# Two-layer graph kernel on one core: node-type embedding products made in the opening stage and kept as six rows, normalised tiles buffered in the place of the second count slab

## Chip, cores and metric

The kernel runs on one core of a Trainium2 chip. The metric is the device time of one execution in microseconds (us). The engines are named PE (TensorE, matmul), PEld (its weight load), ACT (ScalarE), DVE (VectorE), POOL (GpSimd) and SP (SyncE, which only starts DMA transfers). ACT and POOL can start transfers too.

## What is computed

There are 1250 nodes with 768 features, 40000 edges (src, dst, an edge type out of 3) and a node type out of 3. The first block is graph attention with 12 heads of 64, the second one three relational graph convolutions. In front of these the normalised features (768 columns) are joined with an embedding of the node's type (128 columns), so that their first weight matrices have 896 rows.

```
x = layernorm(x + gat(x, W_fc, attn_l, attn_r, W_res, src, dst))
h = concat([x, node_emb[node_type]], -1)                 # 768 + 128
for layer in (1, 2, 3):                                  # rgcn_conv
    xw  = einsum('nd,rde->rne', h, w_rel)                # 3 relations
    msg = xw[edge_type, src] * inv[dst, edge_type]       # inv: 1 / count
    h = relu(segment_sum(msg, dst) + h @ w_root + bias)
x = layernorm(x + h)
```

## The kernel before

It has three stages, and each is a block at whose end the engines meet.

**Counting** (`count_matrices`) turns the edge lists into three matrices of counts, 1250 by 1250, one for each relation, and stores them in DRAM as `ct`. DVE first prepares the edges (keys, one-hot rows `oh_rem`, a table of ranges); when the table has come back through a transfer, PE starts on its windows (L405, L421), and ACT empties them into `ct_stage` (L351). PE transposes some small weights ahead of that (L385 to L392). ACT has nothing to do until the first window is full. Between the small transposes and the first window PE has nothing to do either.

**Attention** (`attention`) runs 12 heads times 10 tiles of 125 nodes. For each of these 120 units DVE, ACT and POOL form the weights `pw` (L774, L687, L692, L647), and PE adds up `head_sums` (L849). At the end of a head ACT copies the sums to `oT`, PE turns them (`turn_sums`, L857), DVE divides (L779 to L784), and POOL adds the result to `res` (L654). `turn_sums` of a head stands behind the sixth unit of the next one. Only for head 10 it stands behind the last unit, directly ahead of that of head 11.

**Relational layers** (`rgcn_layers`) work with float32 matmuls that are split in two parts (high and low): ACT makes the high part (a cast), DVE the low part (a subtraction). So weights `w_raw` become `w_hi` (L1221) and `w_lo` (L1342), and a right-hand side `gs` or `accT` becomes `g_hi` and `g_lo` (L1233, L1364). A step multiplies one block of 128 weight rows with a group of 418 or 416 nodes (`product`, L1101, three matmuls for each 128 outputs). Steps of a relation first sum over the neighbours (`aggregate`, L1073). `STEPS` lists them; in the first group the seven root steps come first, then relation 0, 1, 2. Each engine's program goes through `STEPS` in this order, with the work for a later step written between.

What stands at the head of the layers, before:

- SP loads four blocks `emb_raw` (the last 128 rows of the root and relation weights, L993), then the `w_raw` blocks in order, with two buffers: block j waits for the low part of block j-2 (L1011).
- POOL loads the biases (L1033), then the count slab of relation 0 (`inv` and `ct_in`, L1041, L1043). The second slab's place is at first taken by `emb_raw`, so its load waits for the embedding products. Then POOL stores the ten normalised tiles (L1050).
- PE multiplies `emb_raw` with `emb_cols`, the transposed embedding repeated three times (`embed`, L1110); ACT casts these products to `emb_w` (L1212) and DVE subtracts (L1335) to give the low parts.
- DVE normalises `res` + x, two tiles at a time (`first_norm`: L1304, L1308, L1312, L1314, ACT's square root L1197, L1317, L1324). The results are `x1`, three buffers for ten tiles. A fourth tile waits until the first has been stored.
- For each tile PE transposes `x1` in two halves (`turn_x1`, L1123), ACT keeps them in `accT` (L1206), and ACT and DVE make its high and low part `h_hi` (L1201) and `h_lo` (L1329). Four tiles come before the first step, two more with each of steps 0, 2 and 4. Group 0 needs the first four tiles, and the aggregation needs all ten.

```
if t >= 3:                                   # first_norm: x1 has three places
    dve.wait_ge(x1_out[t % 3], 16 * (t // 3))
```

## Time and profile before

| | us |
| --- | --- |
| median of 3 executions | 2479.14 |
| lowest, highest | 2478.87, 2480.29 |
| the profiled execution, by the clock of the others | 2480.09 |
| its span, first to last instruction | 2478.3 |
| attention, end of the last `res` addition | 814.1 |
| first `product` of the layers | 866.4 |
| first `aggregate` of the layers | 916.3 |

The span is the sum to work with; 1.8 us lie outside it. A row of the timeline names start, length, engine, line, operation and tiles. The square bracket at its end is the idle time of this engine before it and the work that ended it. The chain of work is followed back from the last instruction.

### The profile page before, as it was taken

To read this page: it belongs to the slowest core of one execution; us is meant where nothing else is said; L and a number is where in the kernel's file an instruction comes from. 1 tells how busy PE (TensorE), PEld (TensorE's weight loads), DVE (VectorE), ACT (ScalarE), POOL (GpSimd) and SP (SyncE) were. 2 spreads that over 40 slices of the span, in tenths; PEclk is the share of its full clock that TensorE was granted. 3 is DMA by queue.
4 is the path that set the end of the run, shared out by engine and by line. 5 is a ranking of instruction groups with operands and counts; after the bars stand their busy time and mean duration, and the time that the engine had idled before them with its cause. 6 is when DMAs were issued, how large, how long until landed. Compare 5 with 4: busy or idle time off the path is not lost.

```text
span 2478.3 us, 29974 instructions
## 1 busy us (share of the span) xinstructions
PE 2173.8 (88%) x10953; PEld 1837.3 (74%) x10954; DVE 1228.3 (50%) x1882; ACT 780.9 (32%) x1062; POOL 451.2 (18%) x378
## 2 busy tenths in 40 slices
PE   3998761888888389999999999999999899999997
PEld 1555440333333179999999999999999899999997
DVE  7887656999995452233333342232333342344335
ACT  0133332888886231121221231121221231212212
POOL 0000001899999200000000000000000000000000
PEclk9999885999999589999999999999999999999999
DMA  0133332211110523333423423333323423335332
GB/s 17 42 86 88 89 91 59 89 32 32 32 32 16 159 90 88 99 90 105 121 83 114 113 71 89 97 106 110 117 77 108 123 66 103 121 102 139 100 99 78
DMA packets 138639, 215.04 MB, mean 87 GB/s; under 512 B 87580, under 2 KB 87818, under 8 KB 138513
## 3 DMA queue, kind: packets, MB, share of 16 engines
q1 hardware_dynamic: 99179, 147.28, 21.1%
q0 software_dynamic: 39344, 66.16, 9.3%
q8 instruction: 80, 1.31, 0.2%
q14 instruction: 36, 0.29, 0.0%
HBM read 182.38 MB, written 30.62 MB: 86 GB/s over the span
## 4 chain that ended last, share of the span: by engine, by line
PE 58%; DMA 5%; DVE 2%; ACT 2%; issue 0%; SPq 0%; ACTq 0%; DVEq 0%
PE banks L1101 30%; PE banks L1073 27%; DMA w_raw<-in_L_gnn_w_root_dram 3%; DVE w_lo L1342 1%; ACT w_hi L1221 1%; DMA s_x<-x_tiles 1%; PE banks L1136 1%; DMA emb_raw<-in_L_gnn_w_rel_dram 0%; PE banks L1110 0%; PE banks L1123 0%; PE banks L1154 0%; DVE h_lo L1373 0%; ACT accT L1249 0%; DVE tail_stats L1392 0%; DVE back L1390 0%
## 5 line engine op out<-in xcount | busy, mean ns | idle before, releaser
L1073 PE MATMUL banks<-ct_in,h_hi 125*128 125x416 f32 (+1 forms) x1710 | 604.5, 353 | 0.6 <-ACT accT L1206 0.6
L1073 PE MATMUL banks<-ct_in,h_lo 125*128 125x416 f32 (+1 forms) x1710 | 603.2, 353 | 0.0
L1101 PE MATMUL banks<-g_hi,w_hi 128*128 128x416 f32 (+1 forms) x1440 | 518.4, 360 | 21.6 <-DVE g_lo L1364 21.5
L1101 PE MATMUL banks<-g_lo,w_hi 128*128 128x416 f32 (+1 forms) x1440 | 513.7, 357 | 0.0
L1101 PE MATMUL banks<-g_hi,w_lo 128*128 128x416 f32 (+1 forms) x1440 | 513.4, 357 | 0.0
L1342 DVE TENSOR_TENSOR w_lo<-w_raw,w_hi 128x768 fp32r<-128x768 f32 (+1 forms) x228 | 227.9, 1000 | 468.2 <-ACT w_hi L1221 468.2
L1221 ACT CAST w_hi<-w_raw 128x768 fp32r<-128x768 f32 (+1 forms) x228 | 197.8, 868 | 449.8 <-PE banks L1101 354.6
L1073 PEld LDWEIGHTS banks<-ct_in,h_lo 125*128 125x128 f32 x1710 | 323.7, 189 | 4.4
L1073 PEld LDWEIGHTS banks<-ct_in,h_hi 125*128 125x128 f32 x1710 | 322.5, 189 | 4.1 <-ACT accT L1206 0.8
L1237 ACT CAST g_hi<-gs 128x416 fp32r<-128x416 f32 (+3 forms) x180 | 97.5, 542 | 702.7 <-DVE gs L1352 702.7
L849 PE MATMUL head_sums<-pw,x 125*65 125x512 f32 x720 | 273.0, 524 | 51.5 <-POOL pw L647 35.2
L647 POOL TENSOR_TENSOR pw<-y,csum 125x1250 f32<-125x1250 f32 x120 | 313.9, 2658 | 16.0 <-PE head_sums L849 8.1
L1352 DVE TENSOR_TENSOR gs<-banks,inv 128x416 f32<-128x416 f32 (+3 forms) x180 | 106.6, 592 | 393.4 <-PE banks L1073 393.4
L1101 PEld LDWEIGHTS banks<-g_hi,w_hi 128*128 128x128 f32 x1440 | 276.4, 192 | 29.9 <-DVE w_lo L1342 20.1
L1101 PEld LDWEIGHTS banks<-g_hi,w_lo 128*128 128x128 f32 x1440 | 276.9, 192 | 3.5
L1101 PEld LDWEIGHTS banks<-g_lo,w_hi 128*128 128x128 f32 x1440 | 275.4, 191 | 3.5
L1041 POOL DMA_DIRECT2D inv<-s_inv x27 | 15.4, 571 | 1386.6 <-DVE gs L1352 1373.8
L849 PEld LDWEIGHTS head_sums<-pw,x 125*65 125x65 f32 x720 | 93.4, 139 | 223.8 <-issue 158.9
L294 DVE TENSOR_SCALAR oh_key<-iota_key,edge_cols,minus_window 125x750 bf16<-125x750 uint16 x516 | 212.4, 477 | 79.1 <-PE win L421 55.9
L421 PE MATMUL win<-oh_key,oh_rem 125*128 125x375 bf16 x1032 | 201.9, 341 | 11.4 <-issue 7.8
L774 DVE SCALAR_TENSOR_TENSOR y<-spreads,a_high,low_spread 125x1250 f32<-125x1250 f32 x120 | 180.7, 1516 | 33.5 <-POOL pw L647 21.3
L762 DVE CUSTOM_DVE_ANT_0 junk<-spreads,nbr 125x1250 bf16<-125x1250 f32 x120 | 171.5, 1452 | 32.1 <-PE spreads L816 32.1
(189 smaller groups left out, 1538.5 us busy)
## 6 DMA issues: line engine op xcount, KB each, us to landing
w_raw<-in_L_gnn_w_rel_dram SPq DMA_DIRECT2D x117, 384.0 KB, 3.3
ct_in<-s_ct POOLq DMA_DIRECT2D x18, 2031.2 KB, 28.1
w_raw<-in_L_gnn_w_rel_dram SPq DMA_DIRECT2D x54, 448.0 KB, 3.9
ct_in<-s_ct POOLq DMA_DIRECT2D x9, 2041.0 KB, 28.4
s_ct<-ct_stage SPq DMA_DIRECT2D x30, 610.4 KB
w_raw<-in_L_gnn_w_root_dram SPq DMA_DIRECT2D x39, 384.0 KB, 3.2
w_raw<-in_L_gnn_w_root_dram SPq DMA_DIRECT2D x18, 448.0 KB, 5.8
low_spread<-s_low SPq DMA_DIRECT2D x12, 610.4 KB
```

The lines of the kernel that those rows point to most:

```text
L294: nc.vector.tensor_scalar(oh_key[:, p, b], iota_key[:].rearrange("e s r d -> e (s r d)"), edge[:, 1, bass.ds(c, 1)], minus_w[:, bass.ds(w, ...
L421: ins = nc.tensor.matmul(win[:, p, m, 0:BANK * KEY], oh_rem[:, bass.ds(q, 1), :, b].rearrange("e q s -> e (q s)"), oh_key[:, p, b, m * BAN ...
L647: nc.gpsimd.tensor_tensor(pw[:, u % 3], y[:, u % YS], csum[:, u % NT], ALU.mult).then_inc(weighed, 1)
L762: nc.vector.tensor_tensor_reduce(junk[:, u % 2], a1[:, 0:N], nbr[:, t], 1.0, -NOEDGE / 10, ALU.subtract, ALU.max, tops[:, u:u + 1]).then_i ...
L774: nc.vector.scalar_tensor_tensor(out=y[:, u % YS], in0=r1, scalar=a1_high[:, s, h:h + 1], in1=lowb[:, h % 2], op0=ALU.add, op1=ALU.max).th ...
L849: ins = nc.tensor.matmul(po[:, o:o + w], x[:, s, h], pw[:, u % 3, o:o + w], start=s == 0, stop=s == NT - 1)
L1073: ins = nc.tensor.matmul(pb[0:rows, PA, 0:s.w], a, b, start=j == 0, stop=j == len(pairs) - 1)
L1101: ins = nc.tensor.matmul(pb[:, m, 0:s.w], a, b, start=s.first and j == 0, stop=s.last and j == len(parts) - 1)
L1221: nc.scalar.copy(w_hi[:, s.wi % WS, 0:s.mt * 128], w_raw[:, s.wi % 2, 0:s.mt * 128]).then_inc(w_hi_done, 1)
L1237: nc.scalar.copy(g_hi[0:rows, s.gi % 2, 0:s.w], gs[0:rows, 0:s.w]).then_inc(g_hi_done, 1)
L1342: nc.vector.tensor_tensor(w_lo[at], w_raw[:, s.wi % 2, 0:s.mt * 128], f32(w_hi[at]), ALU.subtract).then_inc(w_lo_done, 1)
L1352: nc.vector.tensor_tensor(gs[0:rows, 0:s.w], pb[0:rows, PA, 0:s.w], inv[0:rows, s.slab % 2, 0:s.w], ALU.mult).then_inc(gs_done, 1)
```

## The change

Six parts.

1. **Embedding products in the counting stage.** ACT loads `emb_raw` (four transfers behind the edge lists). PE transposes the embedding, ACT copies it three times, and PE makes the four products, one for each root or relation matrix, into the PSUM place of the windows. The low part is made by PE and ACT: PE adds minus the high part (`minus_rows`, three rows of minus the identity) onto the product, and ACT casts what is left. Only six rows, three high and three low, are stored to DRAM (`emb`). PE goes on to the windows when the last low part is done.
2. **In the layers** POOL sets `emb_w` to zero, ahead of its first slab load, and SP brings the six rows back in three transfers. The four `emb_raw` loads, `embed` on PE, ACT and DVE, and their waits are gone.
3. **`x1` gets eight places** instead of three: five new ones (`x1_more`) lie where the second slab goes. Only tiles 8 and 9 wait for a place. The second slab's load waits until tiles 3 to 7 are stored, transposed and split. SP stores the tiles, between its weight loads.
4. **Order at the head of the layers.** DVE normalises four tiles in a row; their low parts `h_lo` come behind the first right-hand side. ACT loads the square root table first, and makes `h_hi` of the four tiles behind the first `g_hi`.
5. **The wait for the biases** stands at the first output instead of at the head.
6. **At the end of attention** `turn_sums` of head 10 moves from behind the last unit to behind the sixth unit of head 11. The embedding's load, transpose and copies there are gone.

```diff
@@ count_matrices, scalar @@
+            act.wait_ge(raw_in, 48)
+            for q in range(R + 1):
+                rows = io["L1_gnn_w_root1"][D:D1, :] if q == 0 else io["L1_gnn_w_rel1"][q - 1, D:D1, :]
+                act.dma_start(emb_raw[:, q], rows).then_inc(emb_w_in, 16)
+            act.wait_ge(emb_turned, 1)
...
+            high(0)
+            for q in range(1, R + 1):
+                high(q)
+                low(q - 1)
+            low(R)
...
+            act.wait_ge(emb_out, 32)
             act.wait_ge(consts, 10)
@@ count_matrices, tensor @@
+            products(0)
+            for q in range(1, R + 1):
+                products(q)
+                rest(q - 1)
+            rest(R)
+            pe.wait_ge(emb_low, R + 1)
             pe.wait_ge(u_ready, 4)
@@ attention, tensor @@
-                if h == H - 1 and s == 3:
-                    pe.wait_ge(small_in, 48)
-                    pe.wait_ge(shared, H - 2)
-                    nc.tensor.transpose(turned_emb, emb, ident[0:R, 0:R]).then_inc(emb_turned, 1)
-            pe.wait_ge(emb_kept, 3)
-            turn_sums(H - 2)
+                if s == 5 and h == H - 1:
+                    turn_sums(h - 1)
             turn_sums(H - 1)
@@ rgcn_layers @@
+X1_GROUP = [0] * 3 + [1] * (NT - 5) + [2] * 2
+X1_STORES = {1: (0, 1), 2: (2, 3), 4: (4, 5), 6: (6, 7), 8: (8, 9)}
...
+            nc.gpsimd.memset(emb_w[0:TY].bitcast(F32), 0.0).then_inc(emb_zero, 1)
             load(0)
+            pool.wait_ge(x1_out[1], 16 * X1_GROUP.count(1))
+            pool.wait_ge(xt_turned, 2 * (NT - 2))
+            pool.wait_ge(h_lo_done, NT - 2)
             load(1)
-            for t in range(NT):
-                pool.wait_ge(normed, t + 1)
-                pool.dma_start(dram["x1"][t * T:(t + 1) * T, :], x1[t % 3]).then_inc(x1_out[t % 3], 16)
```

What DVE does at the head of the layers, from the first normalisation on, before (`x1_tiles` and `accT` are the places of `x1`):

```order
L1324 TENSOR_SCALAR x1_tiles<-res,norm_mean_var,norm_var_eps 125x768 x2
L1335 TENSOR_TENSOR emb_w<-banks,emb_w 3x896 x4
L1342 TENSOR_TENSOR w_lo<-w_raw,w_hi 128x896 x2
L1329 TENSOR_TENSOR h_lo<-x1_tiles,h_hi 125x768 x2
L1304 SCALAR_TENSOR_TENSOR res<-res,x 125x768
```

and, further on in the same program, around the first `g_lo`:

```order
L1324 TENSOR_SCALAR x1_tiles<-res,norm_mean_var,norm_var_eps 125x768
L1329 TENSOR_TENSOR h_lo<-accT,h_hi 125x768
L1329 TENSOR_TENSOR h_lo<-x1_tiles,h_hi 125x768
L1364 TENSOR_TENSOR g_lo<-accT,g_hi 128x418
L1342 TENSOR_TENSOR w_lo<-w_raw,w_hi 128x896
```

Now, at the same second place, with the fourth tile's normalisation as the first row:

```order
L1368 TENSOR_SCALAR x1_more<-res,norm_mean_var,norm_var_eps 125x768
L1380 TENSOR_TENSOR w_lo<-w_raw,w_hi 128x896
L1402 TENSOR_TENSOR g_lo<-accT,g_hi 128x418
L1380 TENSOR_TENSOR w_lo<-w_raw,w_hi 128x896
L1373 TENSOR_TENSOR h_lo<-x1_tiles,h_hi 125x768 x2
L1373 TENSOR_TENSOR h_lo<-accT,h_hi 125x768
L1373 TENSOR_TENSOR h_lo<-x1_more,h_hi 125x768
L1380 TENSOR_TENSOR w_lo<-w_raw,w_hi 128x896
L1348 SCALAR_TENSOR_TENSOR res<-res,x 125x768
```

Four `h_lo` moved from ahead of the first `g_lo` to behind it, and stand now ahead of the third weight block's `w_lo`.

SP's transfers at the head of the layers, before:

```order
L993 DMA emb_raw<-in_L1_gnn_w_root1_dram 128x896
L993 DMA emb_raw<-in_L1_gnn_w_rel1_dram 128x896 x3
L1011 DMA w_raw<-in_L1_gnn_w_root1_dram 128x896 x6
L1011 DMA w_raw<-in_L1_gnn_w_rel1_dram 128x896 x36
```

and now:

```order
L1064 DMA w_raw<-in_L1_gnn_w_root1_dram 128x896 x2
L1046 DMA s_x1<-x1_tiles 125x768 x2
L1064 DMA w_raw<-in_L1_gnn_w_root1_dram 128x896
L1068 DMA emb_w<-s_emb 3x3584 x3
L1046 DMA s_x1<-accT 125x768
L1046 DMA s_x1<-x1_more 125x768
L1064 DMA w_raw<-in_L1_gnn_w_root1_dram 128x896 x2
L1046 DMA s_x1<-x1_more 125x768 x2
L1064 DMA w_raw<-in_L1_gnn_w_root1_dram 128x896
```

The first two weight blocks stand at the front, and the third stands behind two stores of `x1`.

## Rows read from the trace of the kernel before

**Rows 1.** Chain that ended last, head of the layers: start us, length us, what

```profile
815.74 9.54 DMA emb_raw<-in_L_gnn_w_rel_dram
825.32 7.61 PE banks L1110 x16
833.01 3.31 ACT emb_w L1212 x4
840.73 21.51 DMA s_x<-x_tiles
...
876.73 6.97 PE banks L1101 x21
896.49 5.58 PE banks L1101 x21
...
916.34 5.63 PE banks L1073 x20
```

**Rows 2.** Timeline of POOL: a memset in attention, bias loads of the layers

```profile
761.39 1.14 POOL L665 MEMSET hot_rows<- 3x1250 f32 x1
...
814.94 2.91 POOL L1033 DMA_DIRECT2D bias_cols<-in_L_gnn_b_dram  x3 [0.85 <-POOLq L508]
```

**Rows 3.** Timeline of the layers' head, DVE, ACT, PE

```profile
824.67 0.96 DVE L1304 SCALAR_TENSOR_TENSOR res<-res,x 125x768 f32<-125x768 f32 x1 [12.19 <-DMA bias_cols<-in_L_gnn_b_dram]
...
828.94 0.17 DVE L1314 TENSOR_SCALAR norm_var_eps<-norm_mean_var 125x2 f32<-125x2 f32 x1
...
838.02 1.28 ACT L1197 ACT_TABLE_LOAD   x1
...
839.75 1.27 DVE L1324 TENSOR_SCALAR x_tiles<-res,norm_mean_var,norm_var_eps 125x768 f32<-125x768 f32 x2
...
847.18 1.82 DVE L1329 TENSOR_TENSOR h_lo<-x_tiles,h_hi 125x768 fp32r<-125x768 f32 x2
...
862.27 0.68 DVE L1324 TENSOR_SCALAR x_tiles<-res,norm_mean_var,norm_var_eps 125x768 f32<-125x768 f32 x1 [7.76 <-DMA s_x<-x_tiles]
...
863.00 1.51 PE L1123 MATMUL banks<-ident,x_tiles 125*128 125x125 f32 x6 [6.92 <-DVE x_tiles L1324]
...
866.37 0.69 PE L1101 MATMUL banks<-g_hi,w_hi 128*128 128x418 f32 x1 [1.86 <-DVE g_lo L1364]
...
866.47 1.09 DVE L1342 TENSOR_TENSOR w_lo<-w_raw,w_hi 128x896 fp32r<-128x896 f32 x1 [0.24 <-ACT w_hi L1221]
```

**Rows 4.** Loads by line or tile: four of `emb_raw`; two of `w_raw`, issued 846 to 848

```profile
DMA to landing us min/median/max: 3.2/5.1/9.5
...
DMA to landing us min/median/max: 9.4/10.4/11.3
```

**Rows 5.** Timeline of the end of attention

```profile
795.95 3.00 DVE L750 TENSOR_SCALAR hot_rows<-nbr,kind_col 64x1250 fp32r<-64x1250 f32 x1
...
801.25 2.31 PE L849 MATMUL head_sums<-pw,x 125*65 125x512 f32 x6 [0.60 <-POOL pw L647]
...
803.40 2.30 PE L857 MATMUL spreads<-wfcT,res 65*125 65x65 f32 x20
...
807.16 4.00 PE L857 MATMUL spreads<-wfcT,res 65*125 65x65 f32 x20 [1.46 <-DVE x L784]
```

**Rows 6.** Loads by tile: four `w_raw` issued 961 to 984, beside a `ct_in` load

```profile
DMA to landing us min/median/max: 3.3/7.2/7.9
```

**Rows 7.** The page's part on DMA issues: tile, queue, count, size, median us to landing

```profile
ct_in<-s_ct POOLq DMA_DIRECT2D x18, 2031.2 KB, 28.1
```

**Rows 8.** Timeline of the counting stage's opening

```profile
6.01 0.94 DVE L206 CAST edges_raw<-edges_raw 80x1500 f32<-80x1500 int32 x1 [5.86 <-DMA edges_raw<-in_edge_type_dram]
...
12.83 0.17 DVE L227 COPY attnT<-scores 64x24 f32<-64x24 f32 x1 [1.36 <-PE scores L389]
...
44.12 0.19 PE L405 MATMUL win<-zero_a 125*128 125x1 bf16 x2 [30.06 <-DVE table L278]
...
66.32 1.28 ACT L351 ACT_TABLE_LOAD   x1 [66.32 <-PE win L405]
```

More of the change, by code:

```diff
@@ L53 @@
 A1_K = 2 * H
+KH = D1 // 128
+TY = 64 + R
 ROWS = [(0, 418), (418, 416), (834, 416)]
 def count_matrices(nc, io, dram, csum, nbr, a1_high, a1_low, a2_col, a_rows, under, stored, proj_out, rows_out, ident):
-    stage, csf, xs, xT, res, iota_key, row, rowp, num = under
+    stage, csf, xs, xT, res, iota_key, row, rowp, num, emb_raw, emb_w = under
     with ExitStack() as ctx:
@@ L393, in _, with products, rest @@
                              start=True, stop=True).then_inc(u_sum, 1)
+            pe.wait_ge(emb_in, 16)
+            nc.tensor.transpose(tp[:, 2, 0:R], emb[:], ident[0:R, 0:R]).then_inc(emb_turned, 1)
+            pe.wait_ge(emb_kept, 3)
+            pe.wait_ge(emb_w_in, 16 * (R + 1))
+            pe.wait_ge(minus_set, 1)
+            half = D1 // 2
+            def products(q):
+                if q >= 2:
+                    pe.wait_ge(emb_low, q - 1)
+                for c in range(2):
+                    ins = nc.tensor.matmul(win[0:TY, q % 2, c, 0:half], emb_cols[:], emb_raw[:, q, c * half:(c + 1) * half],
+                                           start=True, stop=False, skip_group_check=True)
+                ins.then_inc(emb_done, 1)
+            def rest(q):
+                pe.wait_ge(emb_high, q + 1)
+                for c in range(2):
+                    ins = nc.tensor.matmul(win[0:TY, q % 2, c, 0:half], minus[32:32 + R], emb_w[32:32 + R, q, c * half:(c + 1) * half],
+                                           start=False, stop=True, skip_group_check=True)
+                ins.then_inc(emb_rest, 1)
+            products(0)
[4 more added lines that the diff above has]
+            pe.wait_ge(emb_low, R + 1)
             pe.wait_ge(u_ready, 4)
@@ L948, in halves_of_chunk, with rgcn_layers @@
     return ((s.g - 1) * 4 + at // 5, at % 5) if 0 <= at < 20 else None
-def rgcn_layers(nc, io, dram, out, ident, accT, back, emb_w, g_hi, g_lo, gs, bias, hot, hot_rows, emb_cols, many,
-                x, res, h_hi, h_lo, ct, emb_raw, w_hi, w_lo, w_raw, inv, x1_pair):
-    x1 = [x1_pair[:, 0], x1_pair[:, 1], accT[0:T, KX, 0:D]]
+def rgcn_layers(nc, io, dram, out, ident, accT, back, emb_w, g_hi, g_lo, gs, bias, hot, hot_rows, many,
+                x, res, h_hi, h_lo, ct, w_hi, w_lo, w_raw, inv, x1_pair, x1_more):
+    x1 = [x1_pair[:, 0], x1_pair[:, 1], accT[0:T, KX, 0:D]] + [x1_more[:, i] for i in range(NT - 5)]
+    x1 += x1[0:2]
     f32 = lambda ap: ap.bitcast(F32)
@@ L990, in _, with store_x1 @@
         def _(sp):
-            for q in range(R + 1):
-                src = io["L1_gnn_w_root1"][D:D1, :] if q == 0 else io["L1_gnn_w_rel1"][q - 1, D:D1, :]
-                sp.dma_start(emb_raw[:, q], src).then_inc(emb_in, 16)
+            def store_x1(t):
+                sp.wait_ge(normed, t + 1)
+                sp.dma_start(dram["x1"][t * T:(t + 1) * T, :], x1[t]).then_inc(x1_out[X1_GROUP[t]], 16)
             def load_back(c):
@@ L1011, in _ @@
                 sp.dma_start(w_raw[:, j % 2, 0:s.mt * 128], weights_of(s)).then_inc(w_in[j % 2], 16)
+                if j == 2:
+                    sp.wait_ge(emb_zero, 1)
+                    for c in range(3):
+                        sp.dma_start(emb_w[c * 32:c * 32 + R].bitcast(F32), dram["emb"][c % 2]).then_inc(emb_in, 16)
+                if j in X1_STORES:
+                    for t in X1_STORES[j]:
+                        store_x1(t)
                 if s.i == HEADS_OF[2]:
                     for b in range(3):
-                        sp.wait_ge(x1_out[b], 16 * ((NT + 2 - b) // 3))
+                        sp.wait_ge(x1_out[b], 16 * X1_GROUP.count(b))
                     for c in range(4):
@@ L1493, in build @@
         h_lo = t("h_lo", [T, NT, D1], F32R)
-        attention(nc, io, dram, x, res, share, oT, (a1_high, a1_low, a2_col, a_rows), csum, csum16, nbr, y, stored, proj_out, rows_out, (hot, hot_rows, emb_cols, many), ident)
+        attention(nc, io, dram, x, res, share, oT, (a1_high, a1_low, a2_col, a_rows), csum, csum16, nbr, y, stored, proj_out, rows_out, (hot, hot_rows, many), ident)
         ct0 = t("ct_in0", [T, NT, WIDE], F32R)
-        with sb("emb_raw", [128, R + 1, D1], F32) as emb_raw:
+        with sb("x1_more", [T, NT - 5, D], F32) as x1_more:
             pass
```

136 lines of the change are left out of this document (64 added, 72 removed).

## Prediction, written before the changed kernel ran

> **What bounds the kernel now.** I read the chain that ended last first. From 916.34 us on it is PE almost without a break, and this change alters nothing there: the same steps, the same matmuls. Ahead of that the chain leaves PE for a long time, and there the change works. At the head of the layers it goes through the load of `emb_raw` (9.54 us), the embedding products on PE (7.61), ACT's casts of them (3.31), and a store of a normalised tile (21.51) [rows 1]. So from the end of attention at 814.1 (POOL waits 0.85 before 814.94, [rows 2]) to the first product at 866.37 [rows 3] PE has little to do but the work that the change takes out. The reader should see three different waits: DVE's first normalisation waits 12.19 us for the biases, ACT's square root stands behind the casts until 838.02, and the fourth tile waits for the store of the first (7.76 us) [rows 3]. Taking one away would uncover the next; the change takes away all three. So the question is what is late next, and I follow that chain forward.
>
> **The head of the layers, up to the second product.** The engines leave attention at about 814.4 (its own gain comes later).
>
> DVE's statistics of two tiles take from 824.67 to 829.11, 4.44 us [rows 3], so they end at 818.8. ACT splits two weight blocks before the root. These are now SP's first transfers. The four `emb_raw` loads of the same size, which stood there, landed 3.2 us after issue at best and 5.1 in the middle [rows 4], so the second block lands at 819 to 820, its cast (0.85: two of them lie between 833.01 + 3.31 = 836.32 and 838.02, [rows 1, 3]) ends near 820.2, and the root follows. The table load (1.28 us) now runs while the weights are on their way. From the end of the table load at 839.30 to the first tile at 839.75 it is 0.45: tile 0 could start at 820.6.
>
> POOL now sets `emb_w` to zero just there, from 817.85. The nearest row is a memset of 1250 elements in 1.14 us [rows 2]; 3584 elements in proportion make 3.3 us, until 821.1. Does that hurt DVE? A DVE operation of the same form as the normalisation took 3.00 us for 1250 elements beside POOL's work, 2.4 ns each [rows 5]; the normalisation alone takes 0.68 for 768, 0.9 ns each [rows 3]. So such an operation is slowed beside POOL, and I take 0.8 us for it, between 0 and 3.3. The Trainium skill (SBUF — State Buffer, the part on the engine and DMA sides) says that VectorE in a two-port mode and GpSimd hold a common port pair exclusively, the loser waiting for the whole instruction. By that rule tile 0 would start at 821.1 or later, 0.5 us more than without; the slow row agrees with its direction, but its POOL neighbour read memory and a memset doesn't.
>
> Tiles 0 and 1 take 1.27, so 822.7. Then 4.44 for the next two statistics and 0.45 for the root: tile 2 at 827.6, tile 3 at 828.2, DVE free at 828.9. Before, tile 3 started at 862.27 and the first product at 866.37, 4.10 later [rows 3]; now tile 2 is transposed directly ahead of it (1.51 us for a tile, [rows 3]), so the first product comes at 828.2 + 4.1 + 1.5 = **833.8**, 32.6 earlier.
>
> That isn't the gain. The first product was followed by a gap, and the next one came at 876.73 [rows 1], bound by DVE: from the start of the third block's `w_lo` at 866.47 [rows 3] it is 10.26 us. Now four `h_lo` (1.82 for two, 3.64 in all, [rows 3]) stand ahead of that `w_lo`: 833.8 + 1.1 (the second block's `w_lo`, 1.09) + 3.6 gives 838.5 on DVE. The other side is the third block itself. SP issues it when the first `w_lo` is done, 828.9 + 1.1 = 830.0. With a slab load in flight such loads took up to 7.9 us [rows 6], and 9.4 to 11.3 with stores too [rows 4]. Here two `x1` stores stand ahead of it in SP's own queue and the slab (issued at 821.7) is in flight, so I take 8.5: landed 838.5, cast 0.94 later, `w_lo` starts at 839.5, and the second product at **849.8**. That is 26.9 us earlier. Bounds: by DVE alone 848.8 (27.9); without the memset's effect 1 us more (28.9); with 11.3 us of loading 852.6 (24.1).
>
> From the second product to the first aggregation it was 916.34 - 876.73 = 39.6 us [rows 1], with products, transposes and norms in the same order as now. Stores of tiles 4 to 9 went by POOL and go by SP now; the fourth and fifth weight blocks stand behind stores 2 and 3 in that queue while the slab is landing. The fifth one is waited for by ACT in the chain to tiles 6 and 7. I take 0.7 us for it, from 0 to 3. The sum for the head is 26.9 - 0.7 = **26.2** (21 to 29).
>
> What is moved off the path and stays covered: the first slab's load is 3.3 us later and lands about 28 us after 821.7 [rows 7], near 851, against an aggregation at 890; the second slab waits until tile 7 is turned, about 882, lands near 911, and is needed one relation (some 50 us) after 890. The six rows of `emb_w` are needed only with the seventh step. The biases are needed only at the first output. These cost nothing.
>
> **The end of attention.** The last unit's matmuls end at 803.56, then `turn_sums` of head 10 takes 2.30, ACT copies the last head in 1.46 including hand-over, and the last `turn_sums` takes 4.00 [rows 5]. Now the first of these lies behind unit 6. PE has 0.6 us of slack for each unit there [rows 5], so of its 2.3 us some 0.5 are left at the last unit: gain 2.30 - 0.5 = 1.8. The same twenty rows took 2.30 at one place and 4.00 at the other; if the last one keeps the faster pace, 1.7 more. I take the middle, **2.6** (1.8 to 3.5).
>
> **The opening.** PE's windows start at 44.12, behind the range table, after 30.06 us of idling; ACT is idle until 66.32 [rows 8]. ACT's four loads are issued from 6.0 on (the edge lists' arrival, [rows 8]). The same loads took about 10.4 us from the first issue to the last landing (814.4 to 824.8, [rows 1, 4]): 16.5. Four products and four corrections are two matmuls each. PE did eight matmuls of this size in 7.61 [rows 1], so sixteen take 15.2; I allow 24 for a slower pace; ACT's casts are 0.83 each [rows 1], of which three stand in PE's way, since the third product waits for the first low part. 16.5 + 15.2 + 3.3 = 35, at worst 44. The cover ends at 44.12. So its price is **0**, from 0 to 1.
>
> A second cost may hide there: DVE waited 1.36 us, until 12.83, for PE's transposes of the small weights [rows 8], and its work after that runs on to the table. The loads of those weights now share the DMA engines with 1.8 MB. How early they landed no row tells; if they land too late, everything shifts; I take 0, at most 4.
>
> **Sum.** 26.2 + 2.6 + 0 = 28.8 us. The profiled execution took 2480.09 (span 2478.3), 0.95 above the median; its own time becomes 2451.3, and the median 2479.14 - 28.8 = **2450.3**.
>
> **Rivals.**
>
> A, *the weight blocks are late* (chance 0.17). SP's queue carries stores that had been POOL's. If block three lands after 11.3 us and the fifth holds up tiles 6 and 7 by 3 us, the gain is 21 + 2.6: 2455.5. For it speaks the store of 21.51 us [rows 1] in a queue shared with a slab; against it that the slab isn't in this queue now.
>
> B, *more than the sum* (0.13). PE's pace: the product at 876.73 took 6.97 for 21 matmuls, the one at 896.49 5.58 [rows 1]. If one more product goes at the second pace (1.4 us), the last `turn_sums` keeps its own (3.5 in all for the end of attention), the memset costs nothing and no later block is late (28.9 for the head), it is 28.9 + 3.5 + 1.4 = 33.8: 2445.3.
>
> C, *the opening reaches the path* (0.08): small weights late by 4 us or the embedding chain past 44.12. 28.8 - 4: 2454.3, up to 2459 with both.
>
> D, *the gain is given back at the first aggregation* (0.03), if the first slab lands with the aggregation and not 39 us before it. For a gain of zero it would have to land at 890 + 28.8, that is, take 97 us and not 28 [rows 7]: 2479.1, no change.
>
> E, *slower than before* (0.02): the opening chain on PE and ACT as the new bound. It has 14 hand-overs between these engines. To cost more than 28.8 it would have to end at 44.1 + 28.8 = 73 instead of 35, so each hand-over would need 2.7 us more than I count. At 3.2 us each the kernel takes 2486. No row shows such a hand-over: ACT's casts began 0.08 us after the embedding products ended [rows 1].
>
> F, *the change doesn't do what it says* (0.02): some other wait keeps the first root until the late biases or loads; then only the store's wait goes, 7.8 + 2.6: 2468.7.
>
> The forecast's own case has 0.55, 2447 to 2454. The range is 2444 to 2458. About 0.2%, 5 us, is what a measurement of this kernel can tell from no change. Faster by more: all but D, E and a rest, 0.95; same 0.03; slower 0.02.
>
> **What would show it.** In the new profile the first normalisation starts within 1 us of attention's end; tile 0 near 821 minus attention's gain; the first product 32 us earlier, the second 27; the distance from the second product to the aggregation 40. DVE's `w_lo` of the third block waits for ACT's cast by about 1 us. The opening's last cast lies before 44 and the first window where it was. The last `turn_sums` starts about 1.8 us earlier. The sum is wrong if block three lands much later than 8.5 us after issue, if DVE is slow beside the memset, or if the first window moved.

## The result and the profile after

The changed kernel took **2454.41 us** (median of 4 runs, 2453.55 to 2457.33) beside 2479.72 for the kernel before (4 runs, 2478.87 to 2482.09): a ratio of 0.9898, with a 95% interval of 0.9885 to 0.991, so 25.3 us less. In a later measurement it took 2456.31 beside 2478.87, a ratio of 0.9905 (0.9889 to 0.9922), 22.6 us less. Forecast were 28.8 less. The profiled execution has a span of 2451.9 us, against 2478.3 before: 26.4 less, and the working below goes by this pair of traces.

The chain that ended last, in the kernel after, from the end of attention on (start us, length us, what):

```profile
811.05 0.97 DVE res L1348
...
818.02 2.55 DVE x_tiles L1368 x2
...
831.89 24.10 DMA w_raw<-in_L_gnn_w_root_dram
...
858.39 0.95 ACT w_hi L1262
...
870.46 5.37 PE banks L1160 x21
...
890.14 5.61 PE banks L1132 x20
```

Set beside [rows 1]: the loads of `emb_raw`, the embedding products, ACT's casts of them and the 21.51 us store are gone from the head of the layers. The first aggregation starts at 890.14 where it started at 916.34, 26.2 us earlier, which is the whole of the 26.4 in the span: in this pair of traces nothing is given back behind it. In the place of four waits stands one, a load of a weight block that takes 24.10 us from issue to landing.

The timeline of the same stretch, all engines (start us, length us, engine, line, operation, what ended the idle time before it):

```profile
811.05 0.96 DVE L1348 SCALAR_TENSOR_TENSOR res<-res,x 125x768 f32<-125x768 f32 x1 [1.97 <-PEq L575]
...
814.41 3.11 POOL L1104 MEMSET emb_w<- 67x3584 f32 x1
...
815.32 2.22 DVE L1358 TENSOR_SCALAR norm_var_eps<-norm_mean_var 125x2 f32<-125x2 f32 x1
...
816.56 0.94 ACT L1262 CAST w_hi<-w_raw 128x896 fp32r<-128x896 f32 x1 [1.39 <-DMA w_raw<-in_L_gnn_w_root_dram]
817.58 0.20 ACT L1244 ACTIVATE norm_var_eps<-norm_var_eps 125x2 f32<-125x2 f32 x1
...
817.99 2.21 POOL L1101 DMA_DIRECT2D ct_in<-s_ct  x1
...
818.02 2.55 DVE L1368 TENSOR_SCALAR x_tiles<-res,norm_mean_var,norm_var_eps 125x768 f32<-125x768 f32 x2
...
825.98 0.68 DVE L1368 TENSOR_SCALAR x_more<-res,norm_mean_var,norm_var_eps 125x768 f32<-125x768 f32 x1
...
831.01 0.69 PE L1160 MATMUL banks<-g_hi,w_hi 128*128 128x418 f32 x1 [1.86 <-DVE g_lo L1402]
...
839.10 0.94 ACT L1262 CAST w_hi<-w_raw 128x896 fp32r<-128x896 f32 x1 [5.93 <-DMA w_raw<-in_L_gnn_w_root_dram]
...
840.07 1.09 DVE L1380 TENSOR_TENSOR w_lo<-w_raw,w_hi 128x896 fp32r<-128x896 f32 x1 [4.74 <-ACT w_hi L1262]
...
850.05 0.69 PE L1160 MATMUL banks<-g_hi,w_hi 128*128 128x418 f32 x1 [2.43 <-DVE g_lo L1402]
```

All three waits of [rows 3] are gone: DVE's first normalisation step waits 1.97 us where it waited 12.19; the root (ACT L1244) runs at 817.58, directly behind the second block's cast; the fourth tile waits for no store. PE's first two products start at 831.01 and 850.05 where they started at 866.37 and 876.73. What is new: ACT waits 5.93 us for the third block, which landed 11.4 us after its issue. Everything behind it (its `w_lo`, the next two tiles' normalisation, the second product) is as late as this block.

### The profile page after: what moved, and what is told of

It reads as the page before. It is cut to its first block, busy times and chain, and to the rows that moved or that the text cites. A ratio compares the mean times of both kernels' runs of the same rounds, so it can differ in the third digit from the quotient of the medians.

```text
span 2451.9 us, 30026 instructions
## 1 busy us (share of the span) xinstructions
PE 2185.7 (89%) x10969; PEld 1837.1 (75%) x10970; DVE 1227.1 (50%) x1875; ACT 785.2 (32%) x1071; POOL 448.4 (18%) x369
## 4 chain that ended last, share of the span: by engine, by line
PE 58%; DMA 4%; DVE 3%; ACT 1%; issue 0%; ACTq 0%; DVEq 0%
PE banks L1160 30%; PE banks L1132 27%; DMA w_raw<-in_L_gnn_w_root_dram 4%; DVE w_lo L1380 1%; ACT w_hi L1262 1%; PE banks L1184 0%; PE banks L1171 0%; DVE norm_stats L1352 0%; DVE res L1348 0%; PE banks L1202 0%; DVE h_lo L1411 0%; ACT accT L1291 0%; DVE tail_stats L1431 0%; DVE back L1429 0%; ACT accT L1253 0%
## 5 line engine op out<-in xcount | busy, mean ns | idle before, releaser
L710 POOL TENSOR_TENSOR pw<-y,csum 125x1250 f32<-125x1250 f32 x120 | 313.0, 2639 | 16.1 <-PE head_sums L904 8.2
L1160 PEld LDWEIGHTS banks<-g_hi,w_hi 128*128 128x128 f32 x1440 | 275.6, 191 | 32.9 <-DVE w_lo L1380 22.1
L488 PE MATMUL win<-oh_key,oh_rem 125*128 125x375 bf16 x1032 | 201.5, 340 | 11.3 <-issue 8.1
## 6 DMA issues: line engine op xcount, KB each, us to landing
ct_in<-s_ct POOLq DMA_DIRECT2D x9, 2041.0 KB, 28.6
```

Of the source, the lines that this page charges most:

```text
L488: ins = nc.tensor.matmul(win[:, p, m, 0:BANK * KEY], oh_rem[:, bass.ds(q, 1), :, b].rearrange("e q s -> e (q s)"), oh_key[:, p, b, m * BAN ...
L710: nc.gpsimd.tensor_tensor(pw[:, u % 3], y[:, u % YS], csum[:, u % NT], ALU.mult).then_inc(weighed, 1)
L1160: ins = nc.tensor.matmul(pb[:, m, 0:s.w], a, b, start=s.first and j == 0, stop=s.last and j == len(parts) - 1)
```

## The experiments

From the traces of all runs I took two spans, from the first normalisation step (the head of the layers) to the second product and from there to the first aggregation, and two landing times, those of the third and fourth weight block after their issue. The start of the head scatters by some 2 us from run to run of one kernel (811.05 and 812.97 for the changed kernel), because the stages before it scatter; the spans do so far less (39.0 and 39.0; 40.1 and 39.9). So a reason is read from the spans, and the time from the medians. The two needn't agree to the microsecond, because what lies behind the first aggregation varies too. It takes 1558.3 to 1561.3 us in the traces in which the aggregation's first twenty matmuls take 4.09 us at a granted clock of 1.00 (e1, e2, e4, e5, e7, e10), and 1561.6 to 1563.5 us in those in which they take 5.5 to 5.7 us at 0.70 to 0.72 (the kernel before and after, e3, e6, e8, e9, e11).

| kernel | median us | ratio to before (95%) | head to 2nd product | on to aggregation | 3rd block | 4th block |
|---|---|---|---|---|---|---|
| changed | 2454.41 | 0.9898 (0.9885 to 0.991) | 39.0 | 40.1 | 11.4 | 24.1 |
| e8 changed again | 2456.31 | 0.9905 (0.9889 to 0.9922) | 39.0 | 39.9 | 11.4 | 24.4 |
| e1 slab later | 2449.5 | 0.988 (0.9863 to 0.9896) | 32.9 | 40.0 | 3.6 | 11.6 |
| e2 stores later | 2454.46 | 0.9896 (0.988 to 0.9913) | 35.9 | 45.6 | 8.3 | 12.1 |
| e3 rows later | 2452.9 | 0.9888 (0.9871 to 0.9904) | 39.0 | 39.5 | 11.4 | 22.2 |
| e4 memset moved | 2456.13 | 0.9904 (0.9888 to 0.9921) | 42.3 | 39.2 | 16.5 | 23.7 |
| e6 `turn_sums` back | 2458.21 | 0.9919 (0.9902 to 0.9936) | 39.3 | 40.4 | 11.7 | 24.3 |
| e7 opening longer | 2456.41 | 0.9906 (0.989 to 0.9923) | 38.9 | 42.1 | 11.3 | 25.3 |
| e9 parts later | 2454.94 | 0.9898 (0.9881 to 0.9914) | 39.0 | 40.1 | 11.4 | 24.6 |
| e10 slab and parts | 2449.58 | 0.9876 (0.9859 to 0.9892) | 31.1 | 46.1 | 4.8 | 14.4 |
| e11 stores too | 2444.93 | 0.9863 (0.9846 to 0.9879) | 31.1 | 37.9 | 4.7 | 12.6 |

The runs e1 to e4 share one chip and its runs of the kernel before (2480.65), e5 to e7 a second (2478.96), e8 to e11 a third (2478.87). The changed kernel itself ran beside e9 to e11 only, as e8.

### Which transfer makes the third block late: the slab, or the stores

e1: the first slab's load goes behind the third `w_lo`, so that it starts when the third block is there.

```diff
     nc.gpsimd.memset(emb_w[0:TY].bitcast(F32), 0.0).then_inc(emb_zero, 1)
+    pool.wait_ge(w_lo_done, 3)
     load(0)
```

> The changed kernel, but the first count slab is loaded only when the third weight block is split (its low part done); nothing else moves. In the changed kernel the third block landed 11.4 us after issue, the fourth 24.1, the fifth 15.9, all with the slab in flight. Theory 1 (the slab's transfer takes the bandwidth): third block lands in 6 us or less, the second product comes about 4 us earlier (bound by DVE), and the kernel is 3 to 5 us faster than the changed one. Theory 2 (the order in SP's queue, behind stores of normalised tiles): third block still takes 8 us or more, gain under 1.5 us. The slab then lands near 865, ahead of the aggregation near 886.

e2: the slab stays and the first four stores of `x1` go behind the fourth block.

```diff
-X1_STORES = {1: (0, 1), 2: (2, 3), 4: (4, 5), 6: (6, 7), 8: (8, 9)}
+X1_STORES = {3: (0, 1, 2, 3), 4: (4, 5), 6: (6, 7), 8: (8, 9)}
```

> The changed kernel, but SP stores the normalised tiles 0 to 3 behind the fourth weight block instead of behind the second and third. Theory 1 (slab): the third block still takes 8 us or more with the slab in flight, the gain is under 1.5 us. Theory 2 (queue order): the third block lands in 4 to 6 us, the fourth well under 24 us, and the kernel is 3 to 4 us faster; the fifth block may now be the late one, behind four stores, which would take the gain back.

What the loads by tile of `w_raw` say of the third block, issued at 827.5 to 828.3. For e1:

```profile
DMA to landing us min/median/max: 3.6/3.6/3.6
```

and for e2:

```profile
DMA to landing us min/median/max: 8.3/8.3/8.3
```

So of the 11.4 us the slab's absence takes 7.8 off, and the stores' absence 3.1. In e1 the stores of tiles 0 and 1 still stand ahead, issued 7.7 us before the block, and it lands in 3.6 all the same: they delay it only with the slab in flight. Both edits gave the second product earlier, by 6.1 and 3.1 us. But only e1 became faster: 4.9 us less than the changed kernel (5.0 less than e2 and 3.4 less than e3, beside which it ran; and 31.2 less than the kernel before beside it, where the changed kernel is 25.3 and 22.6 less). e2 gave its 3.1 back: its stores have only moved, now ahead of the next blocks, and the chain says so. Chain that ended last, e2, with a row of SP's timeline behind it:

```profile
828.27 8.30 DMA w_raw<-in_L_gnn_w_root_dram
...
844.24 16.33 DMA w_raw<-in_L_gnn_w_root_dram
...
893.09 4.09 PE banks L1132 x20
```

```profile
834.04 10.15 SPq L1046 DMA_DIRECT2D s_x<-x_more  x1
```

The fifth block, issued at 844.24 behind the four moved stores, lands 16.33 us later, and the way from the second product to the aggregation grew from 40.1 to 45.6. It was also issued late. The `w_lo` that it waits for had ended at 838.66, but SP stood for 10.15 us at the issue of the last of the four stores, which takes 0.42 in the kernel after. (That is tile 3, normalised since 827.2, so it didn't wait for its data.) So stores in a row cost the block behind them twice here, 5.6 us before its issue and again in its landing. In e1 there is a late block too, the sixth, which stands behind two stores with the delayed slab in flight:

```profile
845.94 19.95 DMA w_raw<-in_L_gnn_w_root_dram
...
885.10 4.09 PE banks L1133 x20
```

It lands at 865.9 and stands on the chain, yet the way to the aggregation, 40.0, is no longer than in the changed kernel. What the way can be without it e11 tells below: 37.9.

### The three rows of `emb_w`, and the memset

e3 moves the three narrow loads of `emb_w` on SP from behind the third block to two blocks later. e4 sends the slab ahead of the memset, which then runs behind the first two tiles.

```diff
-                if j == 2:
+                if j == 4:
```

> The changed kernel, but the three loads of the six embedding rows (3 partitions of 14 KB each) are issued behind the fifth weight block, not behind the third. If these narrow loads hold up the queue, the fourth block lands in 15 us or so instead of 24.1 and the kernel gains 1 us; if they cost nothing, as I counted in the prediction, the fourth block stays above 20 us and the time is the same within 1 us.

```diff
-    nc.gpsimd.memset(emb_w[0:TY].bitcast(F32), 0.0).then_inc(emb_zero, 1)
     load(0)
+    pool.wait_ge(normed, 2)
+    nc.gpsimd.memset(emb_w[0:TY].bitcast(F32), 0.0).then_inc(emb_zero, 1)
```

> The changed kernel, but POOL starts the first slab's load first (3.1 us earlier) and zeroes the embedding rows only after two tiles are normalised. In the changed kernel DVE's two-element operation beside the memset took 2.22 us and ended with it. Theory M (the memset held up DVE's normalisation): that operation takes 0.2 us, but ACT's casts of the weights ended at the same time, so tile 0 starts at most 0.3 us earlier and the gain is under 1 us. Rival: the memset was on the path with its full 2 us, gain 2 us. The slab's earlier start competes with the first two weight blocks and could cost up to 1 us instead.

e3 changed the fourth block from 24.1 to 22.2 and the third not at all, and its time (2452.9) isn't to be told from the changed kernel's. These narrow loads account for at most 1.9 us of the fourth block. e4 is the more telling one. Its timeline and its chain:

```profile
815.83 2.00 POOL L1101 DMA_DIRECT2D ct_in<-s_ct  x1
...
816.18 1.64 DVE L1359 TENSOR_SCALAR norm_var_eps<-norm_mean_var 125x2 f32<-125x2 f32 x1
```

```profile
826.71 16.52 DMA w_raw<-in_L_gnn_w_root_dram
...
893.37 4.09 PE banks L1133 x20
```

Tile 0 came 0.55 us sooner (6.42 us behind the start of the head, not 6.97). The gain is so small for two reasons. ACT's cast of the second block lasts until 817.98 here, and DVE's two-element step isn't free either: it takes 1.64 us and ends at 817.82, with POOL's issue of the slab (815.83 + 2.00), where it had ended with the memset. So e4 puts one hold-up of this step in the place of another. The slab was issued 3.0 us sooner, counted from the head's start (3.9 us behind it, not 6.9). With that the third block went from 11.4 to 16.5, and the second product came 3.3 us later, where at most 1 was expected. The memset ahead of the slab was protecting the block. It is e1's mechanism, pushed in the other direction. The time, 2456.13, is 3.2 us above e3 beside it, about the size of that step, with intervals that overlap.

### Was the wait for the biases alone worth something

e5 is the kernel before with one edit: the wait for the bias loads moves from the head of DVE's and ACT's programs to the first output that uses them.

```diff
-            act.wait_ge(bias_in, 48)
...
+                act.wait_ge(bias_in, 48)
...
-            dve.wait_ge(bias_in, 48)
...
+                dve.wait_ge(bias_in, 48)
```

> The kernel before, with part 5 of the change alone: the wait for the biases stands at the first output. The prediction held that the waits at the head of the layers lie behind each other: DVE's statistics would be done about 10 us earlier, but ACT's square root still stands behind the casts of the embedding products, so tile 0 starts within 1 us of 839.75 and the kernel is the same within 1 us. Rival: the biases were the head's bound; then it is 8 to 10 us faster.

2479.24 us (10 runs) beside 2478.96 (13 runs), ratio 0.9999 (0.9986 to 1.0012). The chain of its profiled execution is that of [rows 1]:

```profile
818.12 7.80 DMA emb_raw<-in_L_gnn_w_rel_dram
...
842.38 20.17 DMA s_x<-x_tiles
...
914.71 4.09 PE banks L1073 x20
```

DVE's first normalisation starts at 816.82 there, against 824.67 in [rows 3], and little comes of it: the embedding chain and the store bind behind it. Counted from SP's first load (816.77, against 814.39 in the kernel before) DVE starts 10.2 us earlier and tile 0 only 0.7. The forecast's statement that one wait taken away uncovers the next is shown by this run. By the same count the aggregation of this one execution is 4.0 us earlier than in [rows 1], with loads and store that landed a little sooner. The medians don't bear that out: their interval goes from 3.5 us faster to 3.0 slower.

### The end of attention, and the opening

e6 puts `turn_sums` of head 10 back behind the last unit, in the changed kernel.

```diff
-                if s == 5 and h == H - 1:
-                    turn_sums(h - 1)
+            turn_sums(H - 2)
             turn_sums(H - 1)
```

> The changed kernel with part 6 undone: the sums of head 10 are turned behind the last unit again. From the two traces: 2.3 us of transposes come back onto the path, and the last one goes back from 2.4 to 4.0 us, so 3.5 to 4 us slower than the changed kernel. Rival: the moved transposes delayed the units behind them by 0.5 us and the pace was chance; then it is 1.8 us slower.

e7 makes the embedding products in the opening longer: each half of a product is computed twice, with the same result.

```diff
-                for c in range(2):
+                for c in (0, 1, 0, 1):
```

> The changed kernel, with each of the four embedding products in the opening made twice by PE (eight matmuls more, same result). In the changed kernel the chain ended at 42.4 and PE's first window came at 44.45. Eight more take 6 to 12 us. If the cover ends where I put it, near 43.3 (the range table), the first window moves to 50 to 54 and the kernel is 5 to 10 us slower. Rival: the opening has more cover than that, and the time stays within 1 us.

PE's timeline at the end of attention, in the kernel after, and then in e6:

```profile
793.37 2.29 PE L912 MATMUL spreads<-wfcT,res 65*125 65x65 f32 x20
795.50 8.56 PE L904 MATMUL head_sums<-pw,x 125*65 125x512 f32 x24
...
805.36 2.40 PE L912 MATMUL spreads<-wfcT,res 65*125 65x65 f32 x20 [1.29 <-ACT res L764]
```

```profile
802.90 2.30 PE L912 MATMUL spreads<-wfcT,res 65*125 65x65 f32 x20
806.66 3.06 PE L912 MATMUL spreads<-wfcT,res 65*125 65x65 f32 x20 [1.46 <-ACT res L764]
```

With the first `turn_sums` out of the way the last units run without a gap, 24 matmuls in 8.56 us, and the last `turn_sums` starts 1.80 us sooner than in [rows 5] (805.36 against 807.16). It also runs 1.6 us faster, 2.40 instead of 4.00 us for the same twenty matmuls. The cause of that is the granted clock (the last number but two of each row), first in the kernel before and then in the kernel after, over just these twenty:

```profile
807.16:811.16 4.00, 4.00 (x20) 3.81 (x20) 0.00 (x0) 0.00 (x0) 1.47 (x1) 0.56 0.01 4
```

```profile
805.36:807.76 2.40, 2.40 (x20) 2.26 (x20) 0.00 (x0) 0.00 (x0) 0.00 (x0) 1.00 0.00 0
```

In the kernel before, the clock fell from 1.00 to 0.50 (from 2.4 to 1.2 GHz) at 807.6, 0.5 us into the twenty. In the kernel after it fell at 808.4, when they were done. The other two kernels with the old order lie between: it fell 0.7 us into them in e5 (3.80 us, mean 0.59) and 1.5 us into them in e6 (3.06 us, mean 0.74). All ten traces with the new order have 2.40.

How much of this is the edit's? By the starts of the head, e6 (813.01) is 1.96 later than the kernel after, but no later than e8 (812.97), which has the new order: the scatter is as large as the effect. Counted from the end of POOL's last `pw`, which POOL reaches without a gap in its work in either order, SP's first load of the layers comes 10.1 us later in both traces of the changed kernel (800.90 and 802.82), 12.3 in e6 (800.70), 13.0 in e5 and 13.2 in the kernel before (801.20). So the edit brings 2.2 us beside e6 and 3.1 beside the kernel before, and the difference is how early the clock fell. e6 is 20.8 us faster than the kernel before beside it, where the changed kernel is 25.3 and 22.6 faster in its two measurements: by the medians the edit is worth 2 to 4.5 us, with intervals that overlap.

The timeline of the opening, PE and ACT, in the kernel after:

```profile
18.72 5.50 PE L444 MATMUL win<-emb_raw,emb_columns 128*67 128x448 f32 x8 [4.46 <-DMA emb_raw<-in_L_gnn_w_rel_dram]
...
35.21 6.24 PE L451 MATMUL win<-emb_split,minus_rows 3*67 3x448 f32 x8
...
41.48 0.90 ACT L350 CAST emb_split<-win 3x896 fp32r<-3x896 f32 x1 [2.09 <-PE win L451]
...
44.45 0.19 PE L472 MATMUL win<-zero_a 125*128 125x1 bf16 x2 [3.00 <-issue]
```

The chain of products and casts ends at 42.38 (41.48 + 0.90), where 35 was forecast and 44 was its worst case. It came close to its cover's end, 44.12 in [rows 8]. The first window starts at 44.45, 0.33 later, behind "issue" and not behind a cast. In e7's timeline it is behind the cast:

```profile
36.77 4.92 PE L444 MATMUL win<-emb_raw,emb_columns 128*67 128x448 f32 x8 [0.99 <-ACT emb_split L350]
41.62 4.08 PE L451 MATMUL win<-emb_split,minus_rows 3*67 3x448 f32 x8
47.39 0.19 PE L472 MATMUL win<-zero_a 125*128 125x1 bf16 x2 [1.69 <-ACT emb_split L350]
```

Twice the product matmuls put the chain's end at 46.63, 4.3 us later and not the 6 to 12 expected, and the window 2.9 us later, at 47.39. Of that 0.8 is left at attention's first unit (436.76 against 435.96), and the time came out at 2456.41, 2.0 and 0.1 above the changed kernel's two medians; 5 to 10 slower was expected. So the embedding chain as it stands ends close to the edge, and on the path of the window when it is some 2 us longer.

That isn't the whole price, though. The changed kernel's second trace, e8, has its chain's end at 40.73, earlier than the first, and its window 2.2 us later, at 46.65. The store of the six rows, the load of the range table on which the windows wait, and the DVE step that waits for that load, in e8:

```profile
40.76 0.51 ACTq L359 DMA_DIRECT2D s_emb<-emb_split  x1
...
41.29 0.85 SPq L163 DMA_DIRECT2D table_f<-ranges  x1
...
45.50 0.18 DVE L288 CAST table<-table_f 1x50 int32<-1x50 f32 x1 [4.24 <-DMA table_f<-ranges]
```

and the last of these in the kernel after, where the store goes out at 42.41, behind the table's load:

```profile
43.10 0.18 DVE L288 CAST table<-table_f 1x50 int32<-1x50 f32 x1 [2.00 <-DMA table_f<-ranges]
```

Ten traces have this opening as it stands (all but that of e7). In six of them (e2, e3, e4, e8, e9, e10) the store of the rows goes out 1.7 to 0.5 us ahead of the table's load, and the table comes at 44.05 to 45.50, in each 4.7 us behind the store. In the other four (the kernel after, e1, e6, e11) the store goes out 6.9 us or more ahead of the load, or behind it, and the table comes at 42.97 to 43.12, as in the kernel before. The window is late with it, at 45.2 to 46.65 instead of 44.1 to 44.5, and attention's first unit follows: 390.9 to 391.5 us behind the window in all ten. In e8 that unit starts at 437.97, against 435.52 in the kernel before and 435.96 in the first trace of the changed kernel, and this is also the 2 us by which its head is late. So the opening costs 0 to 2.5 us, by whether the new store meets the table's load. This is read from ten traces; no run moved the store.

### The rest of DVE's work, and a faster version

With the block no longer late, DVE is next. e9 moves the four `h_hi` and `h_lo` casts of tiles 0 to 3 from ahead of the steps to behind the split of the second step's operand, so that the third block's `w_lo` no longer waits for them. e10 has both, e1 and e9. e11 moves the stores of tiles 4 to 9 from SP's queue back to POOL's as well.

```diff
-            for t in range(4):
-                low_h(t)
...
+                if s.i == 0:
+                    for t in range(4):
+                        low_h(t)
```

> The changed kernel, with the high and low parts of tiles 0 to 3 (ACT's and DVE's) made behind the second right-hand side, in the gap that DVE has during the second product. The third weight block is still late (slab in flight, stores ahead in the queue). If that load alone sets the second product, as the wait of 4.74 us for ACT's cast says, the time is the same within 1 us. If DVE's four subtractions were on the path, as my sum had as its lower bound, it is 3.6 us faster.

> The changed kernel as it is, for a comparison on one chip with the next three: 25 us faster than before, within 2 us.

> Both: the slab's load behind the third weight block's split (as in the run with the slab later) and the high and low parts of tiles 0 to 3 behind the second right-hand side. With the third block on time DVE is the bound of the second product, so the two add: 5 us for the slab and 2 to 3 us more for the parts, 7 to 8 us faster than the changed kernel. If the fifth and sixth weight blocks, now beside the slab, are late, it gives back up to 5.

```diff
-X1_STORES = {1: (0, 1), 2: (2, 3), 4: (4, 5), 6: (6, 7), 8: (8, 9)}
+X1_STORES = {1: (0, 1), 2: (2, 3)}
...
+            for t in range(4, 8):
+                store_x1(t)
...
+            for t in (8, 9):
+                store_x1(t)
```

> As the run before it, and POOL stores tiles 4 to 9, so that SP's later weight blocks don't stand behind these stores. In the run with the slab later the sixth block took 19.95 us behind two stores with the slab in flight. If that cost time, this is 1 to 4 us faster than the run before it; if it was covered, the same within 1 us.

e9 alone is the changed kernel again in every span (39.0, 40.1) and in the time: as long as the block binds, the order on DVE is free. Together with e1 it takes another 1.8 us off the way to the second product (31.1 against 32.9), and the time stays at 2449.58 (6.7 less than e8 beside it, where 7 to 8 was expected): the way to the aggregation grows from 40.0 to 46.1. The chain of e10, and then of e11:

```profile
831.64 14.44 DMA w_raw<-in_L_gnn_w_root_dram
...
848.19 20.29 DMA w_raw<-in_L_gnn_w_root_dram
...
889.21 4.09 PE banks L1133 x20
```

```profile
825.75 4.71 DMA w_raw<-in_L_gnn_w_root_dram
...
841.42 5.82 PE banks L1170 x21
...
860.02 4.95 PE banks L1170 x21
...
879.29 5.48 PE banks L1142 x20
```

The sixth block is the one that e1 already had late on its chain; in e10 it is issued at 848.19, behind the stores of tiles 4 and 5, with the slab in flight, and lands 20.29 us later. In e11 no store stands ahead of it and it lands after 8.4; the second product comes 31.1 us behind the head's start as in e10, and the aggregation 37.9 behind that. e11 takes **2444.93 us** (2443.81 to 2447.62), 11.4 less than the changed kernel beside it (2456.31) and 0.9863 (0.9846 to 0.9879) of the kernel before. It is the fastest kernel here. (Its first slab landed sooner as well, after 28.6 us instead of 33.1, so not all of the gain need come from the queue ahead of the block.)

## Why the prediction was right, and where it was off

The sign, the size and the range held: 2454.41 lies in 2444 to 2458, 4.1 us above the forecast and 0.4 above the range of the forecast's own case. It lies nearer to rival A (2455.5) than to the forecast, and the traces say why.

**The end of attention**: 2.6 was forecast (1.8 to 3.5) and 3.4 came (814.4 against 811.05), near the upper end. In the pair of traces that is 1.8 for the start of the last `turn_sums`, as in the steps, and 1.6 for its pace, where half of 1.7 stood. The pace hangs on whether the twenty are done before the granted clock falls, and in the new order they are, in ten traces of ten. Without scatter the edit brings 3.1 against the kernel before and 2.2 against e6, so the 2.6 was a fair middle.

**To the first tile**: 6.97 us from the head's start to tile 0, where the steps gave 7.0 (820.6 + 0.8 - 814.4). The 0.8 set for the memset is not what happened, though. A DVE step on two elements a partition, 0.17 us elsewhere, took 2.22 and ended at 817.54, the memset at 817.52. The Trainium skill (SBUF — State Buffer, the part on the engine and DMA sides) has VectorE's two-port operations and GpSimd hold a common port pair one at a time and for the whole instruction; the end times agree with that and not with a slowdown in proportion. It cost little, because ACT's cast of the second block ended at 817.50, and the root had to wait for that anyway; e4, where the slab's issue takes the memset's place beside the step, gained 0.55. The second cost was not forecast. Tiles 0 and 1 were normalised in 2.55 us instead of 1.27, the first in its usual 0.68 and the second in 1.95 (2.55 in seven traces with the slab's issue beside it, 1.27 in e1, e4, e10 and e11 without), while POOL issued the slab (817.99, 2.21 us). That 1.3 us is most of what the fourth tile is late: 14.9 us behind the head's start against 13.8.

**The third block** is the term that was mis-sized most. It was to land 8.5 us after issue, and landed after 11.4, the upper bound of [rows 4] that rival A had taken (11.3). By the path: the block's issue 1.0 later than in the steps (16.6 us behind the head's start, 15.6 forecast), its landing 2.9 later, its `w_lo` 3.9 (29.0 against 25.1), the second product 3.6 (39.0 against 35.4). DVE, forecast as the other side of this race at one microsecond less, waited 4.74. I had both rows, 7.9 with a slab alone and 9.4 to 11.3 with stores too, and took a value nearer to the first, reasoning that the slab was now in POOL's queue and only two stores in SP's. e1 and e2 measure the parts: 3.6 alone, 8.3 with the slab, 11.4 with slab and stores. [rows 4] had this case almost exactly, and was the nearer row.

**From the second product to the aggregation**: 40.3 forecast, 40.1 measured, though by a way I had not drawn. The fourth block landed 24.1 us after issue, not in some 10, and PE's third product waited for it. It cost 0.5 us against [rows 1] (39.6) because that stretch had slack of its own. Rival A's price for later blocks, 3 us, did not come.

**The opening** cost 0.3 us of window in this pair of traces and 2.5 in e8, where 0 to 1 was forecast. Its chain ended at 42.4, between the forecast of 35 and the worst case of 44, and anywhere from 33.4 to 42.4 in the ten traces. The first product started at 18.72, not 16.5 (16.1 to 18.75 over the ten). PE's products and corrections took 20.97 us in six groups, not 15.2. The count was right: the trace writes each matmul as two entries, 16 for the eight of [rows 1] and 32 here. What was off is the pace. 20 of the 32 stand some 0.75 us apart and the others 0.37 to 0.49, and the granted clock was 0.50 in 34 to 42; in e11, at 1.00 nearly to the end, the same 32 took 14.64. What is left for casts in PE's way and hand-overs is 42.38 - 18.72 - 20.97 = 2.7, where 3.3 stood. The small weights were in time: DVE's wait of [rows 8], 1.36 us until 12.83, is there unchanged. But the forecast watched the chain's end alone. It has no term for the store that follows it, and that store is what moved the window in six traces of ten.

The sum in these terms: 28.8 forecast, + 0.8 (end of attention), - 3.6 (to the second product), + 0.2 (from there on) gives 26.2, which is the aggregation's shift. That the third block's 3.6 shows as 2.6 is luck: the end of attention gave 0.8 more than forecast, in part because the clock had fallen early in the kernel before. The medians give 25.3 and, in the second measurement, 22.6. The profiled execution of the second has the late window, and its aggregation comes at 891.84, 24.5 us earlier than before and not 26.2.

**The rivals.** A was right in its mechanism and in its first half. B needed no later block late and a free memset; DVE's 2.2 us beside the memset were covered, but the third block's 2.9 us were not. C came within 2 us of its point of decision by the chain's end, and e7 shows it beyond; something late in the opening did shift everything, up to 2.5 us, but by the store of the rows, which C didn't have. D and E did not occur: the first slab landed 37 us ahead of the aggregation (after 34.9 us, not 28), and the opening ended at 42, not 73. F is excluded by the three waits that are gone. Still open: why the fourth block takes 24 us, when it takes 12.1 with the four stores out of its way (e2) and 11.6 with the slab away for the first 5.3 us of it (e1). It goes with the two together. In all traces that have both ahead of it, it lands only behind the slab, 2.1 to 3.1 us later (6.6 in e4). No run here took its queue apart further.

## What to carry to other kernels

When several transfers are issued together, the one on the path should go first and the bulk one should wait for it: a slab first read 72 us after its issue cost some 5 us of time (3.4 to 8.6 by the comparisons above) by being issued 10 us ahead of a 448 KB block. And when work is moved to where the engines are idle, look also at what its last transfer meets: here the store of six rows delays a small load on the path. Where a trace has a row of a transfer with the same neighbours, take that row and not a kinder one. And an edit that frees one engine shows in the time only when the wait behind it is freed as well; try them in the order of the chain, and try the pair when each alone shows nothing.

## What the runs showed of the hardware

- A 448 KB load on SP's queue landed in 3.6 to 4.8 us with no slab in flight (e1, e10, e11), 8.3 with a 2 MB slab in flight (e2), 11.4 with the slab and two stores ahead (16.5 in e4, with the slab 3.0 us sooner), and 10 to 25 as the fourth or fifth block with both. The sixth block of e10, behind two more stores and beside the slab, took 20.3, and 8.4 in e11 with these stores in the other queue. The slab itself took 34.9 us in the kernel after, 33.1 in e10 and 28.6 in e11.
- SP can stand at an issue. The issue of a 375 KB store took 10.15 us in e2, the fourth of four in a row behind a block with the slab in flight, where it takes 0.42 in the kernel after; that of the fourth weight block took 5.81 in e4, and 0.36 in the kernel after.
- A 50-element load on SP's queue was there 2.0 us after its issue in the kernel before, and after 4.2 us in e8, with a store of 42 KB issued 0.5 us ahead of it on ACT's queue.
- VectorE was held up by GpSimd in two ways: by a memset until its end (2.22 us for a step of 0.17), and by the issue of a transfer on GpSimd's own queue. The latter held the step of two elements until its own end in e4 and e5 (1.64 and 1.67 us for 0.17), and made the second of two normalisations take 1.95 us instead of 0.68.
- Twenty small matmuls behind a gap of 1.3 to 1.5 us took 2.40, 3.06, 3.80 and 4.00 us in four kernels, at a mean granted clock of 1.00, 0.74, 0.59 and 0.56; at 1.00 without a gap they take 2.3. Ahead of the 2.40 PE had run 8.56 us without a pause, ahead of the 4.00 with gaps of 0.6 in every unit; the 3.06 of e6 had gaps of 0.3 and 0.6. The clock fell 0.6 us behind the end of the 2.40 and 0.5 to 1.5 us into the others. What decides the moment of its fall stays open.
